# Two transformer layers on one core: evictions with the division, blockwise norms, filler matmuls and a channel-first scratch tensor

## What is computed

```python
x = x + _L0_conv_ref(_ln_c(x), ...)      # attention in 14 x 14 windows, 12 heads, relative positions
t = t + _L0_ffn_ref(_ln_t(t), ...)       # 8 experts, the best 2 of each token, gelu
x = x + _L1_conv_ref(_ln_c(x), ...)      # dilated 3 x 3 attention, dilations 1, 2, 3
t = t + _L1_ffn_ref(_ln_t(t), ...)       # 8 experts, the best 2 of each token, gelu
```

```python
attn = jnp.einsum('bncl,bnckl->bnlk', qr, kp) * scale
attn = jax.nn.softmax(attn, axis=-1)
out = jnp.einsum('bnlk,bnckl->bnlc', attn, vp)
...
return y @ proj_w.T + proj_b
```

## Time and profile before

| | |
|---|---|
| median of 3 runs | 928.06 us (927.88 to 931.53) |
| profiled execution | 926.22 us |
| its span | 924.4 us |
| TensorE busy | 761.4 us (82%) |
| VectorE busy | 427.2 us (46%) |
| GpSimd busy | 367.6 us (40%) |
| ScalarE busy | 297.6 us (32%) |
| mean granted TensorE clock | 0.876 of full |
| DMA | 96.51 MB, mean 104 GB/s |

### The profile page before, as it was taken

The page is one execution under the profiler, slowest core; times in us unless marked ns, Lnnn a source line. Parts: engine busy times, 40 slices in busy tenths (PEclk is TensorE's granted clock), DMA queues, the critical chain, the costliest instruction groups (busy, mean ns, idle before and its releaser), DMA issues.

```text
span 924.4 us, 19239 instructions
## 1 busy us (share of the span) xinstructions
PE 761.4 (82%) x6098; PEld 668.5 (72%) x6099; DVE 427.2 (46%) x1007; ACT 297.6 (32%) x830; POOL 367.6 (40%) x795
## 2 busy tenths in 40 slices
PE   2999999999891999999981648997682799999990
PEld 1787888888680899999971427883672699999990
DVE  7105545557628333333326305998247433333324
ACT  3222545445523333333331330011210233333330
POOL 5753353330211566666640040000040566676640
PEclk9665899999975899999995778999755899999996
DMA  7382565564581111111103159400861111111115
GB/s 215 104 227 71 127 143 125 141 150 88 173 309 62 45 45 50 44 48 50 50 23 137 30 141 275 68 23 23 301 261 64 40 53 47 47 50 49 46 30 204
DMA packets 63186, 96.51 MB, mean 104 GB/s; under 512 B 28551, under 2 KB 46684, under 8 KB 63136
## 3 DMA queue, kind: packets, MB, share of 16 engines
q1 hardware_dynamic: 42208, 59.60, 22.7%
q0 software_dynamic: 20928, 36.25, 13.1%
HBM read 65.51 MB, written 31.52 MB: 105 GB/s over the span
## 4 chain that ended last, share of the span: by engine, by line
PE 64%; DVE 16%; DMA 6%; issue 5%; POOL 4%; ACT 2%; SPq 1%; DVEq 0%; POOLq 0%
PE ps L1367 14%; PE ps L1375 10%; PE ps L1379 6%; PE ps L735 5%; DMA qkvd<-arena 3%; PE ps L717 3%; PE ps L761 3%; DVE x_sb L1316 2%; PE ps L374 2%; PE ps L745 2%; PE ps L1358 2%; PE ps L1764 2%; PE ps L1746 2%; PE ps L781 2%; DVE arena L1660 2%
## 5 line engine op out<-in xcount | busy, mean ns | idle before, releaser
L1409 ACT ACTIVATE arena<-ps,b1s 128x128 f32<-128x128 f32 x468 | 129.5, 376 | 256.9 <-PE ps L1379 254.1
L1367 PE MATMUL ps<-arena 128*128 x936 | 165.4, 327 | 1.5 <-DVE rt L1281 1.5
L1367 PEld LDWEIGHTS ps<-arena 128*128 128x128 f32 x936 | 150.3, 190 | 2.4 <-issue 2.1
L1375 PE MATMUL ps<-xnT 128*128 128x128 f32 x936 | 120.1, 279 | 3.5 <-DVE xnT L1274 3.5
L1375 PEld LDWEIGHTS ps<-xnT 128*128 128x128 f32 x936 | 116.8, 195 | 4.8 <-DVE xnT L1274 4.8
L270 POOL TENSOR_TENSOR rstd<-veps,cst 128x8 f32<-128x8 f32 (+2 forms) x6 | 10.0, 1659 | 205.0 <-DVE veps L264 205.0
L597 DVE TENSOR_REDUCE rt<-ps 98x2 f32<-98x392 f32 x96 | 52.8, 561 | 78.8 <-PE ps L761 78.8
L1423 POOL TENSOR_TENSOR credit<-credit 1x1 f32<-1x1 f32 x306 | 58.1, 190 | 78.0 <-DVE rt L1281 33.4
L1431 POOL DMA_INDIRECT xnT<-xnd,gcur x78 | 79.1, 1014 | 16.3 <-issue 14.9
L1379 PE MATMUL ps<-xnT,rt 64*128 64x128 f32 x936 | 73.7, 290 | 0.0
L983 ACT ACTIVATE arena<-ps 98x392 f32<-98x392 f32 x96 | 46.9, 499 | 78.4 <-PE ps L781 77.7
(11 more groups left out here) (199 smaller groups left out, 1249.8 us busy)
## 6 DMA issues: line engine op xcount, KB each, us to landing
arena<-in_w SPq DMA_DIRECT2D x16, 576.0 KB, 8.6
arena<-in_w1a SPq DMA_DIRECT2D x16, 384.0 KB, 6.3
arena<-yd SPq DMA_DIRECT2D x8, 768.0 KB, 6.8
kk<-kd SPq DMA_DIRECT2D x48, 96.0 KB
qq<-qd SPq DMA_DIRECT2D x16, 264.0 KB
qd<-arena POOLq DMA_DIRECT2D x16, 224.0 KB, 5.3
qq<-qd SPq DMA_DIRECT2D x16, 192.0 KB
arena<-in_w1b SPq DMA_DIRECT2D x16, 192.0 KB, 6.9
```

What stands on the lines that cost most here:

```text
L1367: last = mm(ps[:, DOWN, 0:C], hidT[r][:, f, :], w2s[:, e, f, :], start=f == 0, stop=f == FT - 1)
L1375: mm(hidden(r, f), wcura[r][:, f * P:(f + 1) * P], xgT[:, 0, :], start=f < 2, stop=False, skip_group_check=True)
L1409: last = nc.scalar.activation(hidT[r][:, f, :], hidden(r, f), ACT.Gelu, bias=b1s[l][:, bass.ds(e * FT + f, 1)])
```

## The change

- `qkvd` has its 16 channels outermost and the columns of `wqkv1` are ordered so that a staged unit is one store: 4 stores a phase instead of 6. SyncE's loads come in another order: k of dilation 3, then, once phase 1 has landed, q and k of dilation 2 and v of dilation 3, then, after phase 2, q and k of dilation 1, v of dilation 2, v of dilation 1.
- The products with v use undivided exponentials. `inverse_sums` only sums and inverts; VectorE evicts the sums from PSUM and multiplies by the inverse (`value_sums`, moved from ScalarE). VectorE's order around it changes, and in each column of the values the single product comes ahead of the pair.
- Both norms around the second attention go block by block. VectorE computes scale and offset (`block_scales`), ScalarE normalises (`block_normalise`), in turn with its copies. `ln_power` runs for each block.
- Filler matmuls whose result nobody reads: nine of 128x512 at the start (the wait for the constants now stands behind them) and two before the third relative part; one of 256 bf16 columns behind each of the 18 units of the first maxima; in each expert stage six behind the ranks and four behind the tables; one a block in the second router; nine before the transposes of the second projection.

```diff
-        qkvd = dram("qkvd", [3 * len(DIL), HD, SPU, GRP, PIX])
+        qkvd = dram("qkvd", [HD, 3 * len(DIL) * SPU, GRP, PIX])
...
+        TURNS += [(2, range(b, b + 1)) for b in range(BLKS)]
+        TURNS += [(3, range(b, b + 1)) for b in range(BLKS)]
...
+        def block_scales(v, n, b):
+
+            ln_refine(v, n, range(b, b + 1))
+            nc.vector.scalar_tensor_tensor(offset[:, b], mv[:, b, :, 0], -1.0, rstd[:, b], ALU.mult, ALU.mult)\
+                .then_inc(s_("ln_offset"), 1)
+
+        def block_normalise(act, n, b):
+
+            act.wait_ge(s_("ln_offset"), (BLKS if n == 3 else 0) + b + 1)
+            if n == 2 and b >= 2:
+                act.wait_ge(s_("xn_free"), b - 1)
+            for j in range(TPB):
+                last = nc.scalar.activation(normed(n, b)[:, j, :], x_sb[:, b * TPB + j, :], ACT.Identity,
+                                            bias=offset[:, b, j:j + 1], scale=rstd[:, b, j:j + 1])
+            last.then_inc(s_("xn_ready" if n == 2 else "nx_ready"), 1)
...
+            filler = rt[:, 2304:2304 + BT]
+
+            def keep_clock(bank, n):
+
+                for _ in range(n):
+                    mm(ps[:, bank, :], filler[:, 0:P], filler, start=True, stop=True)
...
+            pe.wait_ge(s_("filler_ready"), 1)
+            keep_clock(BANK["r2", 0], 9)
+            pe.wait_ge(s_("cst_in"), 16)
...
             queries_and_keys(0, 1)
+            keep_clock(BANK["r2", 0], 2)
             relatives(0, 2)
...
+            pe.wait_ge(s_(EMPTIED["r1", 0][0]), EMPTIED["r1", 0][1])
             for H in range(AHEAD):
                 for u in range(UNITS):
                     scores_for_max(H, u)
+                    mm(ps[:, PV, 0:2 * P], trib, maskb[:, 0, 0:2 * P], start=True, stop=True)
...
-                if l == 0 and b % 2:
+                if l == 0:
                     v.wait_ge(s_("combined"), b + 1)
-                    ln_attn1(v, b // 2)
+                    ln_moments(v, 2, range(b, b + 1))
+                    if b:
+                        block_scales(v, 2, b - 1)
+            if l == 0:
+                block_scales(v, 2, BLKS - 1)
...
-                nx_transpose(pe, l, 0)
                 for b in range(BLKS):
-                    if b + 1 < BLKS:
-                        nx_transpose(pe, l, b + 1)
+                    nx_transpose(pe, l, b)
+                    mm(ps[:, 5, :], ident, cst[:, 0:BT], start=True, stop=True)
                     router_logits(pe, l, b)
...
             last.then_inc(s_("ranks_mm"), 1)
+            for _ in range(6):
+                mm(ps[:, 0, :], ident, cst[:, 0:BT], start=True, stop=True)
...
             last.then_inc(s_("tables_mm"), 1)
+            for _ in range(4):
+                mm(ps[:, 0, :], ident, cst[:, 0:BT], start=True, stop=True)
...
+        UNIT = KC // HD
+        STORES = QKV_UNITS // len(DIL)
...
-            for unit, lo, hi, row in units_of(phase):
+            for k in range(STORES):
+                unit, n = STORES * phase + k, ((2 - phase) * STORES + k) * UNIT
                 eng.wait_ge(s_("qkv_staged"), 2 * unit + 2)
-                to = qkvd[lo // SPU, :, lo % SPU:lo % SPU + hi - lo].rearrange("c b g x -> b c (g x)")
-                eng.dma_start(to, stage[row * HD:(row + hi - lo) * HD, unit]).then_inc(s_(f"qkv_out{phase}"), 16)
+                eng.dma_start(qkvd[:, n:n + UNIT].rearrange("c n g x -> c n (g x)"), stage[:, unit])\
+                    .then_inc(s_(f"qkv_out{phase}"), 16)
 
         def load_qkv(eng, i, t):
 
             d = DIL[i]
             dst = (q1, k1, v1)[t]
-            src = qkvd[i * 3 + t].rearrange("c b g x -> (b g) c x")
+            src = qkvd[:, (i * 3 + t) * SPU:(i * 3 + t + 1) * SPU].rearrange("c b g x -> (b g) c x")
...
             load_qkv(sp, 2, 1)
-            load_qkv(sp, 2, 2)
-            for i in (1, 0):
-                sp.wait_ge(s_(f"qkv_out{position(i)}"), 16 * STORES[position(i)])
-                for t in range(3):
-                    load_qkv(sp, i, t)
+            sp.wait_ge(s_("qkv_out1"), 16 * STORES)
+            for i, t in ((1, 0), (1, 1), (2, 2)):
+                load_qkv(sp, i, t)
+            sp.wait_ge(s_("qkv_out2"), 16 * STORES)
+            for i, t in ((0, 0), (0, 1), (1, 2), (0, 2)):
+                load_qkv(sp, i, t)
...
-            def weights(i):
+            def inverse_sums(i):
                 pos = position(i)
                 v.wait_ge(s_("ex_ready"), pos + 1)
                 vec.tensor_reduce(sm1[i], sc[i].rearrange("p (n x) -> p x n", n=NN), AX.X, ALU.add).then_inc(s_("norm"), 1)
-                v.wait_ge(s_("norm"), 3 * pos + 1)
+                v.wait_ge(s_("norm"), 2 * pos + 1)
                 vec.reciprocal(sm1[i], sm1[i]).then_inc(s_("norm"), 1)
-                v.wait_ge(s_("norm"), 3 * pos + 2)
-                vec.tensor_tensor(by_neighbour(sc[i]), by_neighbour(sc[i]), sm1[i].unsqueeze(1).broadcast_to([P, NN, QPIX]),
-                                  ALU.mult).then_inc(s_("norm"), 1)
-                v.wait_ge(s_("norm"), 3 * pos + 3)
+
+            def value_sums(i):
+                pos = position(i)
+                v.wait_ge(s_("norm"), 2 * pos + 2)
+                v.wait_ge(s_("pv_sum"), (9, 15, 21)[pos])
+                u = SUMS[pos]
+                vec.tensor_tensor(acc[i].rearrange("p (x c) -> p c x", c=HD),
+                                  ps[:, u:u + 2, :].rearrange("p u (c x) -> p (u c) x", x=QPIX),
+                                  sm1[i].unsqueeze(1).broadcast_to([P, HD, QPIX]), ALU.mult).then_inc(s_("acc_ready"), 1)
...
-            def values(i):
+            def values(i, cols=range(3)):
                 v.wait_ge(s_(f"v_in{i}"), 4 * 16)
+                v.wait_ge(s_("ex_ready"), position(i) + 1)
                 if position(i) == 0:
                     for phase in range(3):
-                        v.wait_ge(s_(f"qkv_out{phase}"), 16 * STORES[phase])
+                        v.wait_ge(s_(f"qkv_out{phase}"), 16 * STORES)
                     for n in range(NN):
                         value_product(i, n, next_term()).then_inc(s_("pv_term"), 1)
                     return
-                for col in range(3):
+                for col in cols:
+                    value_product(i, 3 * col + 2, next_term()).then_inc(s_("pv_term"), 1)
                     a_ = next_term()
                     if pairs[0]:
                         v.wait_ge(s_("pv_term"), made[0] - 2)
@@ -1688,23 +1716,26 @@
                     v.wait_ge(s_("pair"), pairs[0])
                     vec.tensor_tensor(in_columns(a_, i, 3 * col), in_columns(a_, i, 3 * col), in_columns(second_term, i, 3 * col),
                                       ALU.add).then_inc(s_("pv_term"), 1)
-                    value_product(i, 3 * col + 2, next_term()).then_inc(s_("pv_term"), 1)
 
             for i in (2, 1):
                 for col in range(3):
                     products(i, col)
             scores(2)
             products(0, 0)
-            weights(2)
             values(2)
+            inverse_sums(2)
             products(0, 1)
             products(0, 2)
             scores(1)
-            weights(1)
+            inverse_sums(1)
             values(1)
+            value_sums(2)
             scores(0)
-            weights(0)
-            values(0)
+            inverse_sums(0)
+            values(0, range(0, 2))
+            value_sums(1)
+            values(0, range(2, 3))
+            value_sums(0)
...
-                if b % 2:
-                    v.wait_ge(s_("proj1_out"), b + 1)
-                    ln_moe(v, 1, range(b - 1, b + 1))
+                v.wait_ge(s_("proj1_out"), b + 1)
+                ln_moments(v, 3, range(b, b + 1))
+                if b:
+                    block_scales(v, 3, b - 1)
+            block_scales(v, 3, BLKS - 1)
...
+            for _ in range(9):
+                nc.tensor.matmul(ps[:, 4, :], ident, cst[:, 0:BT], start=True, stop=True)
...
+            block_normalise(act, 2, 0)
             for b in range(BLKS):
+                if b + 1 < BLKS:
+                    block_normalise(act, 2, b + 1)
                 ln_copy(act, b)
...
-            def value_sums(i):
-                pos = position(i)
-                act.wait_ge(s_("pv_sum"), (9, 15, 21)[pos])
-                u = SUMS[pos]
-                nc.scalar.activation(acc[i].rearrange("p (x c) -> p c x", c=HD),
-                                     ps[:, u:u + 2, :].rearrange("p u (c x) -> p (u c) x", x=QPIX), ACT.Copy)\
-                    .then_inc(s_("acc_ready"), 1)
-
             copy_scores(2)
             exponentials(2)
             copy_scores(1)
-            value_sums(2)
             exponentials(1)
             copy_scores(0)
             exponentials(0)
-            value_sums(1)
-            value_sums(0)
...
+            for b in range(3):
+                copy_values(b)
+            block_normalise(act, 3, 0)
+            copy_values(3)
+            for b in range(BLKS):
+                if b + 1 < BLKS:
```

(43 more changed lines are left out.)

10 lines of the change are left out of this document (1 added, 9 removed).

## The result

The changed kernel takes 900.17 us (median of 4 runs, 897.23 to 901.08), the kernel before, run beside it, 929.36 (927.88 to 931.53): ratio 0.968, 95% interval 0.965 to 0.971. The profiled execution took 897.23 us, its span is 895.4. The forecast was 897, so the median lies 3 us above it. Span against span the gain is 29.0 us where the sum said 30.6.

The account below looks back on a forecast made before the run. Outside the full-clock expert loops, waits and half clock were taken to bound the kernel, the second attention most. Front 4.5, entries 4, combination 2.9, second attention 13.7, router stage 5.5: 926.2 - 30.6 + 1.8 = 897.4, taken as 897; range 884 to 911.

Parts of the forecast that it names:

- Stores: Second attention, phase 0: with 16 channels outermost the last store lands at 531.2 and loads start 12.4 us earlier.
- Loads to first product: Second attention: VectorE's first products start 9.5 us after the loads are issued, between 8 and 10.5, at 540.7.
- beside them run the v loads: Second attention: v loads share the DMA engines with the first loads; putting them later takes 10.5 us to 9.5.
- Division and order of VectorE: Second attention: eviction on VectorE costs 2.0 each, three multiplications go (2.3); last sums leave PSUM at 633.9, not 647.6.
- Combination and first norm: Before the second attention: combining and norming block by block gains 2.9 us (1.5 to 4).
- Projection, norm, router: After the second attention: fillers and the blockwise norm gain 5.5 us, taken between 12 and -1.7.
- One filler a block is thin: Second router: doubt that one filler holds the clock; logits end at 685.2 at full clock, 695.5 at half.
- the rival of the fallen clock: Clock falls anyway: front and router gain 0, loop entries 1, second attention and combination whole; 910 us, chance 0.17.
- Entries: Expert loops' starts: fillers bring full clock to the first up-projection, 1.5 + 0.5 = 2.0 us a loop, 4 in all.
- Front: Start of the kernel, 16 to 68 us, bound by TensorE: fillers gain 4.5 us, from -2 to 9.
- Unspread stores: Rival: phase 0 stores still take about 12 us, second attention gains only 3; 908 us, chance 0.08.
- slow loads: Rival: the layout makes second attention loads 2.5 times as long, costing 22 us there; 933 us, chance 0.03.

Follow-up runs that it names:

- both layout runs: Old scratch tensor layout put back into the changed kernel: 913.24 us, ratio 0.980; new layout alone in the kernel before: 914.34 us, ratio 0.981.
- the kernel with the copy first: The changed kernel with ScalarE's copy of the fourth block of y ahead of the first normalisation: 906.74 us, ratio 0.975.

## Why the prediction was right, step by step

The gain was 1.6 us off span against span; single terms were off by up to 2.6, with signs that cancel, so part of the closeness is luck. The front with the first loop's entry gave 2.6 more than its terms, the way to the first product 2.5 less.

- **Stores.** Right in mechanism and size: the loads start 11.6 us earlier after the first store, 12.4 were forecast, as the last store takes 3.3 and not 2.6. The rule of the Trainium skill, "DMA: Bandwidth & Descriptors", section "Why a DMA increments its semaphore by 16 and not by 1", on the slowest dimension fits the DMA share (29% and 56% over the stores, 0.36, 0.25 and 0.13 in the windows above) and both layout runs.
- **Loads to first product.** Wrong by 1.7: 11.2 us against 9.5. The step that failed is "beside them run the v loads": moving them away freed nothing. What the chain waits for is q of dilation 3 from GpSimd's queue (8.6 after its issue), and meanwhile the DMA engines are full with either order: share 1.17 and 1.20 from 523.3 to 526 and from 526 to 529 us, and 1.17 and 1.20 at the same place with the old order (packets that overlap can make it more than 1). GpSimd issues its eight stores of phases 1 and 2 from 524.0 to 531.8, beside these loads; that they take the place of v is likely, and not run.
- **Division and order of VectorE.** The term for 540.7 to 633.9 was 93.2 us and measured 94.2. The row's price for the eviction was right (1.88 for 2.0), though the output step that "about doubles the time" is a factor of 1.6 by the rows named (1.924 against 2 x 0.595). What was missed is the ring: I let the weighted values start early, and did not ask whether TensorE could take them. They wait 3.5 us, so the head start is gone while VectorE's 1.9 more in this stretch stay.
- **Combination and first norm.** 2.1 for 2.9. A block's normalisation on ScalarE takes 1.86, above the 1.5 taken, within 1.3 to 2.4.
- **Projection, norm, router.** 6.4 for 5.5, and this closeness is luck: 5.5 was a choice between two outcomes, and the clock took the high one (full in all four blocks), for which the prediction had 12 (11.8 before rounding). That was too much by 5.4. The first residual comes 13.5 us after the last eviction, where 11.8 was forecast (1.7). The hold of the last projection by ScalarE was forecast, and to size (10.0 us after the first residual for 10.6), but the projection behind it runs partly cold (1.6). And the full-clock working names a block's transposes and logits (1.0 + 1.7) but not the filler, which stands in the same queue and takes 0.9 of a block's 3.5: from the end of the last projection to the router it is 15.1 us, where the forecast leaves 12.4 (685.2 - 670 - 2.8; 2.7). "One filler a block is thin" was right: it held here, and failed in the kernel with the copy first, where the stage ends as in the rival of the fallen clock.
- **Entries.** First up-projections at 1.60 as forecast, but the loops gained 1.4 and 1.2 where 2 each were given (from the first up-projection to the combination 187.0 instead of 188.5 us; the end in the table). The 0.5 in the forecast's "1.5 + 0.5" did not come: from the router's start to the first up-projection it is 25.1 us instead of 24.8 in the second loop and 24.2 in both kernels in the first. The four fillers hold the transposes of the gathered rows, and nobody waits for these.
- **Front.** 7.6 at the first up-projection, of which the sum had 4.5 and part of an entry. Four kernels without any filler in the front have it at 300.3 to 305.6, nine with all of them at 294.4 to 300.3: 6.6 between the means. The value taken, 4.5 in a range of -2 to 9, was too low by some 2.
- **Rivals.** Unspread stores and slow loads are ruled out by the runs of the layout; the fallen clock in the router happened in other kernels, not in this one's profiled execution.

## What to carry to other kernels

Ask of a slow store first how many pieces its outer dimension gives, before its bytes are counted: one scratch tensor with another outer dimension was worth 12.6 us in the one pair of traces and 13.3 (first store to first load of y) in the other, of 29. When work is moved so that an engine runs ahead, look up the ring or buffer that it fills and who empties it. When fillers are forecast to hold the clock, count their own time too. A filler matmul is part of the order around it: one edit that took a 3 us wait away cost 6, as the clock then fell in the router and stayed down; the same edit with the old division didn't cost it.

## What the runs showed of the hardware

Executions of the same code differ, among other things, by where the clock falls at the end of the first attention. The window from 240 to 270 us (PEclk is the third number from the end), the kernel before, then the one with the layout alone, whose code is the same up to there:

```profile
240.00:270.00 30.00, 24.93 (x251) 20.25 (x250) 15.69 (x65) 13.09 (x28) 7.96 (x8) 0.91 0.92 329
```

```profile
240.00:270.00 30.00, 28.53 (x230) 23.76 (x231) 13.98 (x60) 11.10 (x23) 7.94 (x8) 0.65 0.91 330
```

The first up-projection starts at 302.1 in the one and at 305.6 in the other. The kernel before ran from 924.2 to 935.8 us over all comparisons: this is the width against which a few microseconds have to be read, and why the distances within one trace were used beside the ratios.
